# Low halves of the attention weights: even source tiles to GpSimd, odd ones kept on VectorE

## The reference, cut to what matters

```
def _agnn(x, a, beta):
    x_norm = x / jnp.clip(jnp.linalg.norm(x, axis=-1, keepdims=True), EPS, None)
    scores = beta[0] * (x_norm @ x_norm.T)
    scores = jnp.where(a > 0, scores, NEG_INF)
    attn = jax.nn.softmax(scores, axis=-1)
    return attn @ x
...
h = _leaky(_agnn(x, a, beta1))
h = _leaky(_agnn(h, a, beta2))
return h
```

## Time and profile before

| | before |
|---|---|
| median of 3 executions | 1076.08 us |
| lowest and highest | 1075.3 and 1076.1 us |
| profiled execution, first to last instruction (span) | 1076.3 us |
| TensorE busy | 986.3 us (92%) |
| VectorE busy | 939.5 us (87%) |
| ScalarE busy | 686.1 us (64%) |
| GpSimd busy | 58.3 us (5%) |
| low halves on VectorE (L1043) | 244 instructions |
| low halves on GpSimd (L275) | 12 instructions |

### The profile page before, as it was taken

One profiled execution on the slowest core, in us unless ns is written; L12 is line 12 of the kernel. 1 busy time (PEld: TensorE's weight loads), 2 busy tenths in 40 slices (PEclk: granted clock), 3 DMA queues, 4 the chain that ended last, 5 costly groups with the idle time before them and its releaser, 6 DMA issues.

```text
span 1076.3 us, 20243 instructions
## 1 busy us (share of the span) xinstructions
PE 986.3 (92%) x6624; PEld 625.1 (58%) x6624; DVE 939.5 (87%) x2276; ACT 686.1 (64%) x894; POOL 58.3 (5%) x47
## 2 busy tenths in 40 slices
PE   1889999999967699999999999959999999999995
PEld 1754444444434366666666666636666666666663
DVE  6692888888899989999999999949899999999996
ACT  1721112211235478988989889758878888888784
POOL 0000000000013400000000000000000000000000
PEclk9889999999998899999999999989999999999998
DMA  8328998888852346655565656516566666666600
GB/s 290 113 84 284 296 290 283 282 279 277 282 177 82 118 157 196 196 185 184 187 191 189 195 193 191 189 37 213 180 214 185 207 213 187 215 199 197 211 11 12
DMA packets 107227, 206.38 MB, mean 192 GB/s; under 512 B 3632, under 2 KB 8368, under 8 KB 107184
## 3 DMA queue, kind: packets, MB, share of 16 engines
q1 hardware_dynamic: 105536, 203.44, 59.2%
q0 software_dynamic: 640, 2.10, 0.6%
q10 hardware_dynamic: 1008, 0.33, 0.1%
HBM read 203.75 MB, written 2.10 MB: 191 GB/s over the span
## 4 chain that ended last, share of the span: by engine, by line
PE 43%; DVE 10%; issue 9%; ACT 3%; DVEq 1%; ACTq 0%; POOL 0%; POOLq 0%
PE s_ps L417 20%; PE acc_ps L433 15%; PE acc_ps L435 8%; DVE h_all L1043 5%; DVE work L1036 2%; ACT h_all L650 1%; DVE t L1060 1%; ACT t L683 1%; DVE t L1068 1%; DVE small L1104 0%; DVEq L201 0%; ACT work L643 0%; DVE small L1052 0%; ACT accs L655 0%; DVE small L1102 0%
## 5 line engine op out<-in xcount | busy, mean ns | idle before, releaser
L643 ACT ACTIVATE work<-s_ps,beta_bias,beta_scale 128x1024 f32<-128x1024 f32 x256 | 306.8, 1198 | 76.8 <-PE s_ps L417 76.5
L1036 DVE SCALAR_TENSOR_TENSOR work<-ring,work 128x1024 f32<-128x1024 f32 x256 | 319.8, 1250 | 35.6 <-ACT work L643 32.9
L1043 DVE TENSOR_TENSOR h_all<-work,h_all 128x1024 f16<-128x1024 f32 x244 | 304.7, 1249 | 7.3 <-ACT h_all L650 7.0
L650 ACT ACTIVATE h_all<-work 128x1024 f16<-128x1024 f32 x256 | 268.4, 1048 | 38.5 <-DVE work L1036 37.6
L371 PE MATMUL acc_ps<-ring,set 128*128 128x512 f32 x512 | 224.4, 597 | 3.6 <-DVE set L894 3.6
L433 PE MATMUL acc_ps<-src,h_all 128*128 128x257 f16 x1024 | 190.1, 279 | 21.1 <-POOL h_all L275 10.0
L417 PE MATMUL s_ps<-set 128*128 (+1 forms) x768 | 188.5, 382 | 4.0 <-issue 2.9
L433 PE MATMUL acc_ps<-set,h_all 128*128 128x257 f16 x1024 | 185.2, 274 | 5.4 <-DVE h_all L1043 5.4
L417 PE MATMUL s_ps<-xt 128*128 (+1 forms) x768 | 189.4, 385 | 0.8 <-ACT work L643 0.4
L435 PE MATMUL acc_ps<-src,h_all 128*128 128x129 f16 x1024 | 182.4, 223 | 0.0
L435 PE MATMUL acc_ps<-set,h_all 128*128 128x129 f16 x1024 | 178.5, 221 | 0.0
(11 more groups left out here) (183 smaller groups left out, 680.9 us busy)
## 6 DMA issues: line engine op xcount, KB each, us to landing
ring<-in_adj_t SPq DMA_DIRECT2D x192, 1024.0 KB, 5.5
x_sb<-in_x SPq DMA_DIRECT2D x4, 512.0 KB, 9.5
out<-x_sb POOLq DMA_DIRECT2D x8, 256.0 KB, 3.0
w<-in_layer ACTq DMA_DIRECT2D x2, 64.0 KB, 6.0
w<-in_embed ACTq DMA_DIRECT2D x1, 64.0 KB, 2.8
eb<-in_embed_bias ACTq DMA_DIRECT2D x1, 64.0 KB, 5.2
lb<-in_layer_bias ACTq DMA_DIRECT2D x1, 64.0 KB, 6.7
beta<-in_beta ACTq DMA_DIRECT2D x2, 0.5 KB, 7.9
```

Of the source, the lines that this page charges most:

```text
L643: nc.scalar.activation(e_ring[:, t % ER, :], s_ps[:, t % 2, :], ACT.Exp, bias=beta_bias[:, la:la + 1], scale=beta_scale[:, la:la + 1])\
L650: nc.scalar.activation(ph_ring[:, t % LAG, :], m_ring[:, t % LAG, :], ACT.Copy)\
L1036: V.scalar_tensor_tensor(m_ring[:, t % LAG, :], ring[:, k, half_tile:half_tile + SB, :] .rearrange("p b i -> p (b i)"), 0.0, e_ring[:, t % ...
L1043: V.tensor_tensor(pl_ring[:, t % LAG, :], m_ring[:, t % LAG, :], ph_ring[:, t % LAG, :], ALU.subtract).then_inc(pl_done[la], n)
```

## The change

GpSimd gets a helper `p_lo` of its own with a semaphore `pl_pool`. It makes the low halves of tile 12 of the joined chunk and of every even tile after that, in both layers. VectorE issues `p_lo` only at even `t`, for the odd tile `t - 1`. `wait_p_lo`, used by TensorE and by VectorE's `mask`, chooses the semaphore by the tile's parity. On GpSimd's queue `add_sums` of the former chunk now stands behind the low halves of tiles 0 and 2, and the store of rows behind those of tile 12.

```diff
-        def wait_p_lo(eng, la, n, joined):
-
-            if joined and n <= PAUSES:
-                wait(eng, pl_early, n)
+        def wait_p_lo(eng, la, c, t, joined):
+
+            if t < 0:
+                c, t = c - 1, t + NS
+                if isinstance(c, int) and c < 0:
+                    return
+            if joined and t < PAUSES:
+                wait(eng, pl_early, t + 1)
+            elif t % 2:
+                wait(eng, pl_done[la], c * (NS // 2) + (t // 2 + 1))
             else:
-                wait(eng, pl_done[la], n)
+                wait(eng, pl_pool[la], c * (NS // 2) + (t // 2 + 1))
...
+            def p_lo(la, c, t, n=1):
+                pool.wait_ge(ph_done[la], c * NS + (t + 1))
+                wait(pool, pv_done[la], c * NS + (t + 1 - LAG))
+                pool.tensor_tensor(pl_ring[:, t % LAG, :], m_ring[:, t % LAG, :], ph_ring[:, t % LAG, :],
+                                   ALU.subtract).then_inc(pl_pool[la], n)
+
             pool.wait_ge(flags, 1)
             with pool.If(pool.value_load(beta_big[0:1, 0:1]) == 0):
...
+                p_lo(0, 0, PAUSES, PAUSES // 2 + 1)
...
-                with pool.Fori(0, NC) as c:
-                    add_sums(la, c)
-                    if la == 1:
-                        pool.wait_ge(out_ready, c + 1)
-                        pool.dma_start(out_v[:, ds(c * CB, CB), :], x_sb[:, ds(c * CB, CB), :]).then_inc(stored, 16)
+                with pool.If(pool.value_load(beta_big[0:1, la:la + 1]) != 0):
+                    for t in range(0, PAUSES + 1 if la == 0 else 2, 2):
+                        p_lo(la, 0, t)
+                if la == 1:
+                    with pool.Else():
+                        p_lo(1, 0, 0)
+                for t in range(PAUSES + 2 if la == 0 else 2, NS, 2):
+                    p_lo(la, 0, t)
+                with pool.Fori(1, NC) as c:
+                    p_lo(la, c, 0)
+                    p_lo(la, c, 2)
+                    add_sums(la, c - 1)
+                    for t in range(4, NS, 2):
+                        p_lo(la, c, t)
+                        if la == 1 and t == 12:
+                            rows_out(c - 1)
+                add_sums(la, NC - 1)
+                if la == 1:
+                    rows_out(NC - 1)
...
-                wait_p_lo(dve, la, c * NS + (t + 1 - LAG), joined)
+                wait_p_lo(dve, la, c, t - LAG, joined)
...
-                    if t > t0:
-
-                        p_lo(la, c, t - 1, 1 + t0 if t == t0 + 1 else 1)
-                    elif not first:
+                    if t > t0 and t % 2 == 0:
+
+                        p_lo(la, c, t - 1, 1 + t0 // 2 if t == t0 + 2 else 1)
+                    elif t == 0 and not first:
                         p_lo(la, c - 1, NS - 1)
```

More of the change, by code:

```diff
@@ L175, in build @@
         pl_early = sem("pl_early")
+        pl_pool = [sem(f"pl_pool{i}") for i in range(2)]
         pv_done = [sem(f"pv_done{i}") for i in range(2)]
@@ L286, in add_sums, with rows_out @@
                     .then_inc(summed[la], 1)
+            def rows_out(c):
+                pool.wait_ge(out_ready, c + 1)
+                pool.dma_start(out_v[:, ds(c * CB, CB), :], x_sb[:, ds(c * CB, CB), :]).then_inc(stored, 16)
             for la in range(2):
@@ L293, in _ @@
                     else:
-                        pool.wait_ge(pl_done[0], NC * NS)
+                        pool.wait_ge(pl_done[0], NC * NS // 2)
+                        pool.wait_ge(pl_pool[0], NC * NS // 2)
                         pool.wait_ge(ph_done[0], NC * NS)
@@ L424, in weighted_sum @@
             def weighted_sum(la, c, t, joined=False):
-                wait_p_lo(pe, la, c * NS + (t + 1), joined)
+                wait_p_lo(pe, la, c, t, joined)
                 if t == 0:
```

## The result

The changed kernel takes 1148.15 us (median of 4 executions, 1146.25 to 1149.52). The kernel before, on the same chip, takes 1075.69. The ratio is 1.0669 with a 95% interval of 1.0654 to 1.0684: 72 us slower. The forecast was 1164, in a range of 1136 to 1206. The profiled execution has a span of 1147.6 us, 71.3 more than before; its own time was 1149.52, so about 1.9 us lie outside the span. The remark ahead of the prediction that nothing measurable lies around the span set two different executions side by side, and doesn't hold. It doesn't touch the difference.

A forecast was written before the change was run, and what follows sets the result against it. TensorE bounds layer 1 and alternates with VectorE in layer 0; after the change the VectorE-GpSimd pair would bound both. Chunks 64.4 + 0.8 + 1.8 and idle 21 make 88 us on 1076.3: 1164 us, range 1136 to 1206.

The forecast's parts named there:

- price of 1.95 us per turn: VectorE's queue: each low half made by GpSimd costs 1.95 us there, against 1.14 when VectorE makes it, adding 0.81.
- Idle time on top: Attention chunks of both layers: idle time of the VectorE-GpSimd pair adds 7 x 2 + 7 x 1 = 21 us.
- `add_sums`: Each chunk's sums on GpSimd: their 1.27 us falls into a never idle queue, less 0.17, costing 1.1 us.
- The tail of chunk 0 of layer 0: Only tiles 12 and 14 move there; each costs the difference of lengths in latency, 2 x 0.9 = 1.8 us.
- chunk 0 of layer 1: Without a former chunk's work, the pair needs 43.0 us against TensorE's 42.2, adding 0.8.
- the bounds: Whole kernel: 1141 us with no idle time; 1214 with a 2.12 us slot and more idle; forecast's own bounds 1141 to 1195.
- rival 2: TensorE's clock falls after idle stretches, once per chunk: 34 us on top, 1198 us; chance 0.12.
- rival 3: GpSimd works beside VectorE after all, leaving TensorE alone the bound: 10 us gained, 1066 us; chance 0.04.
- rival 1: VectorE's idle time absorbs GpSimd's turns, so chunks grow by perhaps half: 35 us more, 1111 us; chance 0.10.
- 51 and 48 us: Sign in the changed profile: chunk periods expected in layer 0 and layer 1.
- below 47 us: the price of a turn is wrong: Sign in the changed profile: chunk periods under 47 us would mean the price of a turn was wrong.
- near 85%: Sign in the changed profile: TensorE's busy share within chunks, waiting for low halves and for exponentials.

The follow-up runs named there:

- The extra subtractions: Kernel before plus one GpSimd 128x1024 subtraction per two tiles of layer 1, on data nobody else uses, with no engine waiting; 1176.92 us, ratio 1.0959.
- the run with no even low halves: Changed kernel with all of GpSimd's new `p_lo` calls taken out, so even tiles' low products use old contents; 1059.88 us, ratio 0.985.
- the run with `add_sums` behind the first wait: Kernel before plus GpSimd memsets in layer 1, `add_sums` ahead of tile 2's memset but behind the wait for its high half; 1084.0 us, ratio 1.0075.
- the copy: Kernel before plus one GpSimd 128x1024 float32 copy, one SBUF input, per two tiles of layer 1; 1108.15 us, ratio 1.03.

## Why the prediction was right, and where its sizes were off

**The mechanism held.** GpSimd's low halves and VectorE's instructions run one at a time, and the pair of them became the bound. The price of 1.95 us per turn was read from the 12 early tiles. In layer 1 of the changed kernel it can be solved for: 46.74 less 24 x 1.14, 3.0 and 0.7 for `add_sums` leaves 15.7, 1.96 each; with the 0.5 us taken off in which neither engine works, 1.90. The extra subtractions gave it again, 55.95 against 55.8.

**The difference of 16 us** is made up by stage. Between the profiled executions, from the sum of columns to the last `add_sums` of layer 0 are 361.1 us (383.23 to 744.33) instead of 315.8: +45.3. The forecast had 7 x 7.0 + 1.8 = 50.8. From there to the last `add_sums` of layer 1 are 393.7 us instead of 364.4: +29.3, where the forecast had 37.2. The rest is small: the stages up to the first mask, from there to the sum of columns, and after the last `add_sums` were 1.1, 1.4 and 0.8 us shorter. Together that is 71.3. The sum of columns is a moving mark: on VectorE the even low half ahead of it is gone, which puts it about 1 us earlier. By the masks, the first of chunk 1 of layer 0 starts 1.4 us earlier than before (386.72 against 388.15), and from there to the last `add_sums` of the layer 44.2 us are added, where the forecast had 7 x 7.0 = 49.0.

The terms that were off:
- *Idle time on top*, 21 us. This is the mis-sized term. In layer 1 nothing of the 1 us per chunk came. ScalarE's wait for the sums is there, 1.6 us long where about 1 was forecast, but VectorE's idle time falls beside GpSimd's turns, as at 893.86. From the records, the time in which neither of the two engines works is 0.5 us in that chunk, where it was 2.0 before the change. Adding it to a sum that already counts the turn counts it twice. In layer 0 the period is 1.6 us above the sum (50.57 against 49.0, see the next term) and not 2.0; neither engine works for 1.5 us of it, as much as before the change. In all 11 us instead of 21.
- *`add_sums`*, 1.1 us per chunk. It costs 0.7, since it falls beside small instructions. With that the sums are 49.0 and 46.7, and 14 chunks are 6 us less.
- *The tail of chunk 0 of layer 0*, +1.8. Nothing of it is seen: the next chunk's first mask even starts 1.4 us earlier, as said.

The other way went chunk 0 of layer 1. From the last mask of layer 0 (694.71 before, 736.74 now) to the first mask of chunk 1 of layer 1 (761.83 and 806.39) 2.5 us are added, where 0.8 were forecast. Why it is 1.7 more wasn't traced, and some 1 us of the whole isn't placed.

Two slips in the bounds changed nothing: 1141 leaves the 1.8 of the tail out (1143 with it), and the upper bound is once 1214 and once 1195.

**TensorE's clock** (rival 2) stayed at 1.00 in all chunks shown, though TensorE was idle for 6 us of 50. **GpSimd working beside VectorE** (rival 3) is refuted for instructions that read SBUF and true for memsets beside the masks and low halves. Its size was also low, 10 us for what measured 16: layer 0 comes down to 42.95, not 43.4. **Idle time absorbing the turns** (rival 1) has the same error seen from the other side: some idle time does fall beside turns, but the measured 1148 lies above its 1085 to 1141, since the turns need over 15 us of a chunk and no idle time of that size was there.

**Signs in the profile.** Of those named, 134 subtractions and records near 3 us came. Of VectorE's masks and low halves in the attention chunks, 70 of 361 are stretched and not one in three, and most of them to 1.9 to 2.3 us; 3.0 comes 7 times. The other turns fell on small instructions or, as at 892.98, partly on idle time of VectorE's. "51 and 48 us" came as 50.6 and 46.7; the mark of "below 47 us: the price of a turn is wrong" was met in layer 1, and it was wrong as a mark, because the price was right and the idle term was not. TensorE's share was given as near 85%, and is 88% and 93% (44.48 of 50.57, 43.29 of 46.74). These busy times are 1.6 and 1.0 us above those of the run with no even low halves, for the same products, so the share understates the stall.

## What to carry to other kernels

Before work is moved from VectorE to GpSimd, look in the trace for one place where both run at once, and take the distance between VectorE's starts there: what GpSimd's instruction adds to it is the price, to be set against what VectorE saves. Here a GpSimd subtraction took 1.95 us of VectorE's queue to save 1.14, so each move lost, and undoing 12 old ones won 8 us. A GpSimd memset is another matter: it cost nothing beside VectorE instructions with two SBUF inputs. And a sum of the pair's work is a lower bound. It was good in layer 1 where it lay well above TensorE's 42.2 us (55.8 for 55.95, 46.7 for 46.74), and 1.2 us too low there where it lay just above (43.4 for 44.63); in layer 0 it was 1.6 to 2.4 us too low.

## What the runs showed of the hardware that I had not expected

- A GpSimd memset of 1.81 us didn't touch VectorE's instructions with two SBUF inputs: a period of 42.95 us with eight of them per chunk, against 42.93 without.
- The same memsets did hold VectorE's tiny `TENSOR_SCALAR`s over 128x4 float32 with one SBUF input. In the run with `add_sums` behind the first wait, they had means of 0.76 and 0.70 us instead of 0.16, and ended with the memset (902.51 + 1.80 = 904.31; 903.58 + 0.76 = 904.34):

```profile
902.51 1.80 POOL L318 MEMSET src<- 128x2048 f32 x1
```

```profile
903.58 0.76 DVE L1068 TENSOR_SCALAR zero<-accs 128x4 f32<-128x4 f32 x1
```

- The price was below the 2.12 us of GpSimd's own record for two small reasons. GpSimd's subtraction ended 1.99 us after the mask that it had waited for (892.98 to 894.97). And the held VectorE instruction ended 1.08 us after that (896.05), where two VectorE instructions in a row end 1.14 apart. 1.99 + 1.08 - 1.14 is 1.93. For the copy it was 0.84 us of 1.15, of which 0.17 had gone by before VectorE's instruction started.
- The place of a short GpSimd instruction can matter more than who waits for it: `add_sums` held VectorE for 0.7 us beside small instructions and for 1.1 beside a full tile's, while the removal of ScalarE's 1.6 us wait for it gained nothing.
